# Masked cross attention: maxima over two banks at once, scores through a ring of three banks, K in three pieces, divisions at the end

## What is computed

```
q = split_heads(query @ Wq.T + bq)          # 16 heads, 256 queries of 16
k = split_heads(key @ Wk.T + bk)            # 4096 keys of 16
v = split_heads(value @ Wv.T + bv)
scores = q @ k.T / sqrt(16)
scores = where(mask, scores, -1e9)
p = softmax(scores, axis=-1)
out = merge_heads(p @ v) @ Wo.T + bo
```

## Time and profile before

| what | value |
|---|---|
| time, median of 3 runs | 721.85 us (721.85 to 725.36) |
| time of the profiled execution | 717.97 us |
| its span from first to last instruction | 715.4 us |
| PE busy (matmul) | 612.3 us, 86% |
| ScalarE busy | 456.7 us, 64% |
| VectorE busy | 407.2 us, 57% |
| share of the DMA engines, queue q1 | 34.8% |
| mean granted clock of PE | 0.976 of 2.4 GHz |
| the second cross attention, first score matmul to last probability matmul | 375 to 563 us |

### The profile page before, as it was taken

The page is one execution under the profiler, slowest core; times in us unless marked ns, Lnnn a source line. Parts: engine busy times, 40 slices in busy tenths (PEclk is TensorE's granted clock), DMA queues, the critical chain, the costliest instruction groups (busy, mean ns, idle before and its releaser), DMA issues. The chain is left out here.

```text
span 715.4 us, 14402 instructions
## 1 busy us (share of the span) xinstructions
PE 612.3 (86%) x4946; PEld 365.9 (51%) x4946; DVE 407.2 (57%) x899; ACT 456.7 (64%) x541; POOL 67.4 (9%) x151
## 2 busy tenths in 40 slices
PE   1698858878878879795679999999999999898998
PEld 0353424444444445463435555555555575574786
DVE  6567371322223134876389898989896226645644
ACT  3889969999999994683027676767676414603111
POOL 3000101100001100101031212121211000000000
PEclk9999989999999999999789999999999999999999
DMA  5786766556534313203602333332231390000000
GB/s 133 217 241 228 215 198 194 146 182 188 155 103 113 92 44 99 66 2 110 199 3 79 84 80 83 80 84 78 83 80 29 101 297 1 2 1 1 0 1 15
DMA packets 52832, 73.46 MB, mean 103 GB/s; under 512 B 10979, under 2 KB 29731, under 8 KB 52795
## 3 DMA queue, kind: packets, MB, share of 16 engines
q1 hardware_dynamic: 52027, 72.25, 34.8%
q10 hardware_dynamic: 768, 0.73, 0.4%
HBM read 58.90 MB, written 12.85 MB: 100 GB/s over the span
## 5 line engine op out<-in xcount | busy, mean ns | idle before, releaser
L1631 DVE TENSOR_REDUCE sb_m_blk<-ps 128x1 f32<-128x512 f32 x256 | 159.5, 684 | 18.9 <-PE ps L1476 17.7
L1412 ACT ACTIVATE sb_probs<-ps 128x1024 f32<-128x1024 f32 x128 | 125.8, 1024 | 50.0 <-PE ps L1506 49.7
L655 ACT ACTIVATE sb_probs<-ps 128x1024 f32<-128x1024 f32 x128 | 124.0, 1016 | 15.8 <-PE ps L701 13.4
L659 ACT ACTIVATE sb_probs<-sb_probs,sb_neg_cap,sb_cap 128x4096 f32<-128x4096 f32 x32 | 121.6, 3801 | 1.1
L718 PE MATMUL ps<-sb_probs,sb_v_st 128*32 128x256 f32 x1024 | 76.5, 395 | 39.5 <-ACT sb_probs L659 36.8
L701 PE MATMUL ps<-sb_q_st,sb_k_st 112*128 112x256 bf16 x512 | 75.7, 283 | 5.8 <-DMA sb_k_st<-k_parts_l 3.6
L1506 PE MATMUL ps<-sb_q_st,sb_k_st 115*128 115x256 bf16 x512 | 76.4, 272 | 1.5 <-ACT sb_probs L1412 1.5
L1476 PE MATMUL ps<-sb_k_st,sb_q_m 96*128 96x512 bf16 x224 | 76.6, 383 | 0.0
L701 PEld LDWEIGHTS ps<-sb_q_st,sb_k_st 112*128 112x128 bf16 x512 | 46.0, 100 | 48.9 <-ACT sb_probs L655 24.1
L1522 PE MATMUL ps<-sb_probs,sb_v_st 128*32 128x256 f32 x1024 | 67.4, 384 | 0.2 <-ACT sb_probs L1412 0.2
L718 PEld LDWEIGHTS ps<-sb_probs,sb_v_st 128*32 128x32 f32 x1024 | 24.0, 110 | 68.0 <-ACT sb_probs L659 45.0
(11 more groups left out here) (282 smaller groups left out, 824.0 us busy)
## 6 DMA issues: line engine op xcount, KB each, us to landing
sb_k_st<-k_parts_l SPq DMA_DIRECT2D x223, 64.0 KB, 2.0
sb_k_st<-k_parts_l SPq DMA_DIRECT2D x93, 128.0 KB, 3.2
k_parts_l<-sb_v_proj SPq DMA_DIRECT2D x24, 256.0 KB
k_parts_l<-sb_early SPq DMA_DIRECT2D x48, 128.0 KB
sb_v_proj<-ctxT_blocks SPq DMA_DIRECT2D x8, 512.0 KB, 8.4
sb_early<-ctxT SPq DMA_DIRECT2D x7, 512.0 KB, 3.8
sb_v_rows<-ctx_by_pair SPq DMA_DIRECT2D x7, 512.0 KB, 4.2
sb_k_st<-k_parts_l SPq DMA_DIRECT2D x64, 32.0 KB, 1.8
```

The costliest lines, as they stand in the source:

```text
L655: a.activation(probs[:, j % 2, 4 * g:4 * g + 4, :], scores_bank(g), ACT.Tanh).then_inc(s["tanh"], 1)
L659: a.activation(probs[:, j % 2], probs[:, j % 2], ACT.Exp, bias=k.neg_cap[:, 0:1], scale=k.cap[:, 0:1]).then_inc(s["exp"], 1)
L1412: sc.activation(probs[:, g], scores_bank(g), ACT.Exp).then_inc(s["exp"], 1)
L1631: v.tensor_reduce(k.m_blk[:, b, q, blk:blk + 1], k.ps[:, m_bank(m_turn_of(idx)), :], AX.X, ALU.max).then_inc(s["m_read"], 1)
```

## The change

- The maximum pass writes two banks (1024 keys) for 128 queries with two matmuls, and one reduction reads both. There are eight reductions for a head in place of sixteen, in two pairs of banks (4, 5 and 6, 7), and the ring is two deep. The number of matmuls and their 96 rows stay.
- The score pass works in pieces of one bank (two matmuls), sixteen for a head, through banks 0, 1 and 2. The exponential reads one bank. Probability matmuls still work in groups of two pieces and write bank 3. `sel` writes bank 0 and `m_turn` bank 2, which they borrow from the ring between two pieces.
- ScalarE copies the sums of `sel` to a tile `o_raw`. VectorE divides for fifteen heads at once after the last of these copies, and for head 15 by itself.
- K comes in three pieces: two of 1024 keys and one of 2048 keys. The pieces are released after 4, 8 and 16 score pieces of the head two before. The maximum pass waits for them at its pairs 0, 2 and 4, the score pass at pieces 0, 4 and 8.
- PE's order is new, as listed in the diff.

```diff
+PIECES1 = ((0, QUARTER), (QUARTER, QUARTER), (UNIT_KEYS, UNIT_KEYS))
...
-    M_AHEAD = 4
-    ACC_BANK, M_BANK, M_BANKS = 4, 5, 3
+    M_AHEAD = 2
+    ACC_BANK, M_BANK, FIRST_BANK = 3, 4, 4
+    SCORE_BANKS = (0, 1, 2) + tuple((u + 1) % 3 for u in range(3, units))
+    SUM_BANK, TURN_BANK = 0, 2
+    BEFORE = {0: -2, 1: -1, 3: 1, 4: 2} | {u: u - 3 for u in range(6, units)}
...
-                    for quarter in range(4):
-                        sp.wait_ge(s["scores"], 16 * it - 16 + 8 * b + 2 * (quarter + 1))
-                        load_k1_quarter(k, sp, 2 * it + b, b, quarter, k_in[b][quarter])
+                    for piece in range(3):
+                        sp.wait_ge(s["scores"], 2 * units * it - 2 * units + units * b + (4, 8, 16)[piece])
+                        load_k1_piece(k, sp, 2 * it + b, b, piece, k_in[b][piece])
...
-                if idx % 4 == 0:
-                    pe.wait_ge(k_in[b][quarter], 16 * K_LOADS1 * (it + 1))
...
+                if idx in (0, 2, 4):
+                    pe.wait_ge(k_in[b][idx // 2], 16 * K_LOADS1 * (it + 1))
+                if not (begin and b == 0 and idx < 2):
+                    pe.wait_ge(s["m_read"], n_m * h + idx - 1)
...
+                if u in (0, 4, 8):
+                    pe.wait_ge(k_in[b][u // 4], 16 * K_LOADS1 * (it + 1))
+                if u == 5 and not (first and b == 0):
+                    pe.wait_ge(s["o_read"], h)
+                elif u in BEFORE and (u > 1 or not (first and b == 0)):
+                    pe.wait_ge(s["exp"], units * h + BEFORE[u] + 1)
...
             def pv(h, b, g, first):
-                pe.wait_ge(s["exp"], groups * h + g + 1)
+                pe.wait_ge(s["exp"], units * h + 2 * g + 2)
...
+                        m_next(0)
+                        m_next(1)
                         if behind:
-                            pv(h - 1, 1 - b, groups - 2, not before)
-                            pv(h - 1, 1 - b, groups - 1, not before)
-                        m_some(0, 1)
+                            pv(h - 1, 1 - b, groups - 2, False)
+                        if behind:
+                            pv(h - 1, 1 - b, groups - 1, False)
                         qk(it, b, 0, masked, first)
-                        m_some(1, 4)
                         qk(it, b, 1, masked, first)
-                        m_some(4, 5)
                         qk(it, b, 2, masked, first)
-                        m_some(5, 6)
+                        m_next(2)
+                        if behind:
+                            sel(h - 1, 1 - b)
+                        m_next(3)
+                        qk(it, b, 3, masked, first)
+                        qk(it, b, 4, masked, first)
+                        qk(it, b, 5, masked, first)
                         pv(h, b, 0, not behind)
                         pv(h, b, 1, not behind)
...
+                        qk(it, b, 6, masked, first)
+                        m_next(4)
+                        m_next(5)
+                        qk(it, b, 7, masked, first)
+                        qk(it, b, 8, masked, first)
+                        qk(it, b, 9, masked, first)
                         pv(h, b, 2, not behind)
                         pv(h, b, 3, not behind)
...
+                        qk(it, b, 10, masked, first)
+                        qk(it, b, 11, masked, first)
+                        m_next(6)
+                        m_next(7)
+                        qk(it, b, 12, masked, first)
+                        qk(it, b, 13, masked, first)
                         pv(h, b, 4, not behind)
                         pv(h, b, 5, not behind)
+                        qk(it, b, 14, masked, first)
+                        qk(it, b, 15, masked, first)
                         if not (last and b == 1):
                             m_turn(*((it, 1) if b == 0 else (it + 1, 0)))
```

More of the change, by code:

```diff
@@ L1320, in pairs_of_heads, with m_banks, m_beside @@
         body(H // 2 - 1, False, True)
[L1322 to L1331, removed]
-        else:
-            exists, head, idx0 = not last, (it + 1, b), M_AHEAD - n_m
-        return [(head[0], head[1], idx0 + n) for n in range(n0, n1)] if exists else []
+    sums_of_parts = k.ps[:, SUM_BANK, 0:32 * QT].rearrange("p (q n) -> p q n", q=QT)
+    def m_banks(idx):
+        return slice(M_BANK + 2 * (idx % 2), M_BANK + 2 * (idx % 2) + 2)
+    def m_beside(it, b, n, last):
+        if n < n_m - M_AHEAD:
+            exists, head, idx = not (last and b == 1), ((it, 1) if b == 0 else (it + 1, 0)), M_AHEAD + n
+        else:
+            exists, head, idx = not last, (it + 1, b), M_AHEAD + n - n_m
+        return (head[0], head[1], idx) if exists else None
     with nc.Block() as block:
@@ L1460, in m_scores @@
                 blk, q = divmod(idx, QT)
-                quarter = idx // 4
+                rows = k.q_st if first and h < 2 else k.q_m
                 if idx == 0 and begin:
@@ L1567, in body, with m_next @@
                         behind = not (first and b == 0)
-                        before = behind and not (first and b == 1)
-                        def m_some(n0, n1):
-                            for x in m_beside(it, b, n0, n1, last):
-                                m_scores(*x, masked, first)
+                        def m_next(n):
+                            at = m_beside(it, b, n, last)
+                            if at:
+                                m_scores(*at, masked, first)
+                        m_next(0)
@@ L1686, in body @@
                 for b in range(2):
-                    h = 2 * it + b
-                    for mit, mb, idx in m_beside(it, b, 0, SEL_TURN, last):
-                        m_read(2 * mit + mb, mb, idx)
-                        if idx == n_m - 1:
-                            m_all(2 * mit + mb, mb)
-                    if not (first and b == 0):
-                        normalise(h - 1, 1 - b)
-                    for mit, mb, idx in m_beside(it, b, SEL_TURN, n_m, last):
-                        m_read(2 * mit + mb, mb, idx)
+                    for n in range(n_m):
+                        at = m_beside(it, b, n, last)
+                        if at:
+                            m_read(2 * at[0] + at[1], at[1], at[2])
+                            if at[2] == n_m - 1:
+                                m_all(2 * at[0] + at[1], at[1])
             pairs_of_heads(dve, body)
-            normalise(H - 1, 1)
+            normalise()
+            normalise_last()
 def load_late_weights(k, sp):
```

155 lines of the change are left out of this document (71 added, 84 removed).

## The result

The change makes the kernel slower: 746.48 us median of four runs (744.85 to 750.71) against 721.85 us of the kernel before beside them (719.46 to 725.36). The ratio is 1.0359, with a 95% interval of 1.0305 to 1.0413. The forecast was 745 us, slower.

The account below looks back on a forecast made before the run. TensorE was taken as full, then waiting for the long K piece in each head: 14 heads at 1.71 us give 23.9, plus 1.3 at the start and 0.2 in the last head, 25.4; forecast 745 us, range 731 to 758.

Parts of the forecast that it names:

- The bound: Second cross attention: TensorE issues almost without a gap, 11.76 of 11.91 us a head; helping VectorE or ScalarE gains at most 0.15.
- Maxima over two banks at nothing: VectorE's maximum pass: eight reductions of 1024, each at most 1.26 us, replace sixteen of 512; no cost, covered by full TensorE.
- Scores through three banks at nothing: ScalarE's exponentials: 16 of 512 a head, about 9 us with copies, below TensorE's time; no cost, bounds 0 to 0.2 us.
- TensorE's order, 12.28 us: TensorE's work in a head: 11.76 us plus 0.52 for two more changes to 32-column matmuls and back.
- the trip: TensorE going from full-width matmuls to the 32-column form and back; priced at 0.26 us from the rows.
- a full drain: TensorE emptying at each tiling-mode switch: 0.16 us each way, 0.32 a round trip; would add 1.8 us to rival 3.
- The K piece, 13.62 us: Load of K's second half: 4.20 us from release to use against 2.86 of cover; TensorE waits 1.34, head 13.62.
- the two halves of the loop: K piece's use to next first load issued, 9.42 plus 0.17 us; from that issue to use, 3.93 plus 0.1.
- Ends: Start and last head of the second cross attention: 1.3 us more at the start, 0.2 in the last head, bounds -1 and +1.
- The walk's 1.3: Start: two maximum pairs of head 1 ahead of the first scores put the first score matmul at 376.4, not 375.08.
- rival 1: K's long piece lands as fast as a quarter, 1.7 us after fourth issue: head 12.82, 732 to 736 us; chance 0.13.
- Clock: TensorE's clock expected at 1.00; rival 5 had each new wait lower it, 3.5 us each, about 793 us; chance 0.03.

Follow-up runs that it names:

- spread order: Changed kernel, only TensorE's order within a head altered: fifth maximum pair further behind its K release, few-column work in three stretches, not five; 721.38 us, ratio 0.9984.

## Why the prediction was right, and where not

**The bound.** TensorE full before, and next to nothing to gain from VectorE: shown. Half of the maxima's work removed gives 0.12 us a head; the prediction had said at most 0.15.

**Maxima over two banks at nothing.** Shown in the spread order: 1.22 us each, under the bound of 1.26, and no change of the head when halved.

**Scores through three banks at nothing.** No run undoes this part alone. Kernels that contain it run at a full TensorE (11.70 and 12.23 us, the second equal to the sum of rows and trips), so no cost of it shows while ScalarE copies the sums. What the prediction missed is that the ring of three makes the sums' bank a score bank, and so needs that early copy. It had priced the divisions as work of VectorE (nothing), which is right for the change as it is only thanks to that copy.

**TensorE's order, 12.28 us.** Measured 12.23 with the K wait gone; the trip 0.24 for 0.26. TensorE's rows without the waits were good to 0.05 us. By the rows a full drain would be 0.32 a trip; 0.24 was measured for one more trip, and 0.53 for two fewer. The Trainium skill, TensorEngine Tiling (Array Packing), Key Properties, says that a switch of the tiling mode drains the engine; both measured prices lie somewhat under the 0.32.

**The K piece, 13.62 us.** Each link was met: eight distances of 13.54, 9.56 and 4.04 us for the two halves of the loop, the landing 2.4 to 2.5 us behind the issue of the fourth load as in the first cross attention, though the rows were twice as long. From landing to matmul it was 0.12 us (466.44 to 466.56) for the estimate of 0.1. A quarter in the same place waits 0.5 us, and more distance takes the wait away with the same piece. This was the term that decided, and it is shown from three sides.

**Ends.** The last head: 10.62 us (585.30 to 595.92) for 10.6. The start was the weak term. It is 15.90 us from the first maximum matmul to the first scores where it had been 13.99, so 1.9 in place of 1.3. But with four quarters in the same order, which changes nothing there, it is 14.36, 0.4 more than before; with one of them late it is 15.90 again. In both traces of 15.90 a stretch at the low clock begins 1.1 us ahead of the first scores (380 to 387 us above), and in that of 14.36 the clock is 1.00 from 371 us on. So the two pairs ahead of the scores cost 0.4 us where the clock stays up. The walk's 1.3 was too much, and by the terms that it names (372.9, twice 1.26 and a pair of 0.44) it comes to 375.9 and not 376.4.

Head 0 the prediction left at its old length. It was 11.53 us before and 12.48 with four quarters in the change's order; in the change's profiled run it took 14.46, with the clock at 0.51 from 380 to 387 us.

**The sum.** From head 1 on, 14 heads pay, but the last of them only 1.26 (12.40 for 11.14). Thirteen times 1.63 and this 1.26 are 22.5, where 23.9 was forecast. The start's 0.4, head 0's 1.0 and the last head's 0.2 make 24.0; the medians say 24.6, the prediction said 25.4. So the mechanism is right and the closeness of the total is in part luck: the heads and the start were put too high, and head 0 at nothing. The range's low end, 731, stands 1 us under the 732 of rival 1's own sum, which changes nothing here.

The profiled pair differs by 8 us more than the medians. Of these, 4.1 lie ahead of the stage, where nothing changed; most of the others are the clock at the start, and the heads 1 and 3, which took 14.3 each. An explanation drawn from this pair alone would have found 8 us too many.

**Clock.** It did not fall in the change's heads from 387 us on, as forecast. With one wait of 0.51 us more in each head it fell in four heads of fifteen.

## What to carry to other kernels

When a load may start only behind the last reader of its buffer, set the work between that release and the first use against the time from release to landing; one longer load in place of two moves the release back and the landing out, and an order that uses it later can give nearly all of it back (25 us here, of which some 8 are the two trips that this order saves). A buffer in a ring comes free when its last reader has run, so a small operation can cost TensorE the rest of a long one that it queues behind, even on an engine that is idle for a third of the time.

## What the runs showed that I had not expected

- A trip from full-width to 32-column matmuls and back costs about a quarter of a microsecond at 2.4 GHz: one more, 0.24 us a head; two fewer, 0.53, where one of the two is that of the small turn.
- The divisions of 0.35 us cost 0.86 us a head behind a maximum of 1.22 us, on a VectorE with 2 us of slack.
- A wait of 1.15 to 1.41 us in each head left the clock at 1.00 from 400 to 550 us. With 0.5 us of waiting more in each head it fell to 0.50 for about 3 us in four heads of fifteen; the three of them in the steady part took 1.5 us more.
- Time is 543.5 us and 15 heads, within 1 us, for nine of the eleven kernels with steady heads, the two given included. Two are off. 541.9 (divisions in the spread order) is within the 3.4 us of its time's interval; 540.1 (half maxima in the kernel before) goes with a gain of 4.9 us of which the traces show 2.3.
